# Masked attention block on one core: inverse roots placed apart from their scalings, Q or K ahead of three output projections, V finished in slot 4, and a quarter of the square moves made by ScalarE

## Chip, core and metric

The kernel runs on one core of a Trainium2 chip. The metric is device microseconds of one execution. The engines are named as in the profile: PE (TensorE), PEld (its weight loads), DVE (VectorE), ACT (ScalarE), POOL (GpSimd), SP (SyncE, which issues all DMAs here).

## The reference, cut to what matters

```python
# x: (8, 1024, 384) f32, adj: (8, 1024, 1024) bool, 6 heads of 64
q = heads(x @ Wq + bq); k = heads(x @ Wk + bk); v = heads(x @ Wv + bv)
scores = einsum('bhqd,bhkd->bhqk', q, k) / sqrt(64)
probs = softmax(scores + where(adj, 0.0, -9e15), axis=-1)
ctx = einsum('bhqk,bhkd->bhqd', probs, v)          # merged to (8, 1024, 384)
out = layernorm(x + ctx @ Wf + bf)                  # over the last axis, no affine
```

## The kernel before

Products of full precision are made as three products of a high and a low part in F32R (`three_products`). Each batch (1024 tokens) is cut into 24 slots. A slot `s` makes the scores of one block of 128 queries against all 1024 keys for one pair of heads. Two slots (an even and the following odd one) make a group: 256 queries, one pair of heads; a batch has 12 groups, and three groups (the three pairs of heads) make one row block of 256 tokens.

In a slot PE writes the scores of two heads to `score_ps` (`scores`). DVE adds the mask and finds the row minimum (`mask_scores`, two instructions, one for each head; the text calls the first of them the slot's mask), ACT takes the exponential in place in `prob` (`exponential`), and DVE transposes each 32x32 block in place (`turn_squares`). For the product with V the whole matrix has to be transposed, so after the group's odd slot the 4x4 squares of 32 partitions by 1024 elements are moved from `prob` to `prob_t`, from partitions 32a to partitions 32c (`move_square`, 16 DMAs for a group; `move` issues them in two halves). Each adds 16 to the semaphore `landed[group % 2]`; at 256 the group is complete. Both buffers are double: group g uses half g % 2. So the mask of the next slot that writes that half, slot 2g+4, waits for `landed`, and so does `mix(g)`.

`mix(g)` (32 products on PE into `context_ps`, which line 514 of the profile shows) stands in slot 2g+4, except that group 0 comes in slot 5. Before it stands job `i`: PE spreads the inverted row sums over a PSUM bank (line 436) and ACT copies them to `context`, ahead of the slot's exponentials (`evicted_early`). After the mix DVE multiplies (`divide`), ACT rounds to the high part (`context_high`, line 612), POOL forms the low part (`context_low`, line 805); the output projection `p` of a tile needs these.

What PE does in each slot beside the scores is written out by hand in the table `STEADY`: `("kind", number, piece, ahead)`, with kinds `q`, `k`, `v` (projections), `x` (transposes of the next batch's x), `i`, `m` (mix) and `p` (output projection). `ahead` 1 is work for the next batch, a negative number belongs to the batch before. Jobs take three PSUM banks in turn (`bank_free`). ACT evicts the jobs in the same order behind the exponentials: for `q`, `k` and `x` a high part and a copy `raw` (two halves in turn), from which POOL forms the low part (`low_part`). All engines run the same table in order, each waiting on semaphores. Other tables say in which slot SP loads and stores (`STORES`, `RES_LOADS`, `X_LOADS`), where POOL adds the bias to the residual rows (`RESIDUALS`), and where POOL normalises (`NORMALISE`): there `normalise` makes 12 small steps for the inverse root and then `scale_rows` two instructions of 128x384, at the end of POOL's work of the slot.

Of the kernel before, what the change touches and what calls it, by code (L numbers as in the profile page):

```python
# [11 lines left out]
ACT = mybir.ActivationFunctionType  # L12
# [8 lines left out]
ROOT_OPS = 4 * NEWTON_STEPS  # L21
# [41 lines left out]

STORES = {1: -2, 9: -1, 13: 0, 19: 1}
RES_LOADS = {2: 0, 10: 1, 14: 2, 20: 3}
X_LOADS = {4: (0, 0), 6: (0, 1), 11: (1, 0), 12: (1, 1)}
RESIDUALS = {6: 0, 13: 1, 17: 2, 23: 3}
NORMALISE = {0: -2, 8: -1, 12: 0, 18: 1}

# [25 lines left out]
def slots_of(mode):  # L95
    return range(SLOTS + 2 if mode == "last" else SLOTS)


def evicted_early(mode, s):

    jobs = [w for w in slot_work(mode, s) if w[0] != "m"]
    return jobs[:1] if jobs and (jobs[0][0] == "i" or s == 5) else []


def contexts_split(mode, s):

    groups = [w[1] for w in slot_work(mode, s) if w[0] == "m" and SPLIT_LATER.get(s) != w[1]]
    return [SPLIT_LATER[s - 1]] + groups if s - 1 in SPLIT_LATER else groups


# [6 lines left out]
def graph_attention(nc, x, adj, wq, bq, wk, bk, wv, bv, wf, bf, out):  # L117
# [15 lines left out]
    with ExitStack() as ctx:  # L133
# [181 lines left out]
        def _(sp):  # L315
# [26 lines left out]
            def move(b, group, part):  # L342
                if part == 0:
                    sp.wait_ge(squared, at(b, UNITS, 4 * group + 4))
                    sp.wait_ge(mixed, at(b, GROUPS, group + 1))
                for a in (2 * part, 2 * part + 1):
                    for c in range(4):
                        move_square(sp, group, a, c)

# [207 lines left out]
        def _(act):  # L557
# [42 lines left out]
            def exponential(b, t):  # L600
# [6 lines left out]
                                     accum_out=row_sum[:, s // 2 % 2, col:col + 1]).then_inc(exp_done, 1)  # L607

            def context_high(b, group):
                act.wait_ge(context_done, at(b, GROUPS, group + 3))  # L610
                act.wait_ge(projected, at(b, TT, 2 * ((group - 4) // 3) + 6))
                nc.scalar.activation(context_hi[:, group % 4, :], context[:], ACT.Copy).then_inc(context_hi_done, 1)  # L612

            def body(b):
                for s in slots_of(b.mode):
                    early = evicted_early(b.mode, s)
                    for job in early:
                        evict(b, job)
                    if s < SLOTS:
                        exponential(b, 2 * s)  # L620
                        exponential(b, 2 * s + 1)
                    if s - 1 in SPLIT_LATER:
                        context_high(b, SPLIT_LATER[s - 1])
                    for job in slot_work(b.mode, s):
                        if job[0] not in "pm" and job not in early:
                            evict(b, job)
                    for group in contexts_split(b.mode, s):
                        if s - 1 not in SPLIT_LATER:
                            context_high(b, group)
# [17 lines left out]
        def _(dve):  # L647
# [71 lines left out]
            def body(b):  # L719
                for s in slots_of(b.mode):  # L720
# [11 lines left out]
                    for job in work:  # L732
                        if job[0] == "p":
                            add_residual(b, job)
                            moments(b, job[1])

            weights = 0
# [27 lines left out]
        def _(pool):  # L765
# [41 lines left out]

            def normalise(b, group):
                pool.wait_ge(guess_done, at(b, 4, group + 1))
# [9 lines left out]
                for _ in range(NEWTON_STEPS):  # L819
# [3 lines left out]
                    result(nc.gpsimd.tensor_tensor(guess, guess, newton[:], ALU.mult))  # L823
                scale_rows(nc.gpsimd, group)

            def body(b):
                for s in slots_of(b.mode):
                    work = slot_work(b.mode, s)
                    for job in work:
# [9 lines left out]
                    for group in contexts_split(b.mode, s):  # L839
                        context_low(b, group)  # L840
                    if s in RESIDUALS:
                        residual(b, RESIDUALS[s])
                    if s in NORMALISE and (NORMALISE[s] >= 0 or b.mode != "first"):
                        normalise(b, NORMALISE[s])
                    if s == SLOTS:
                        normalise(b, 2)
                    if s == SLOTS + 1:
                        normalise(b, 3)

# [35 lines left out]
```

## Time and profile before

| what | value |
|---|---|
| median of 3 runs | 1355.2 us (1343.33 to 1359.98) |
| profiled execution | 1353.83 us, its span 1352.0 us |
| PE busy | 1196.9 us, 89% |
| DVE busy | 1057.4 us, 78% |
| ACT busy | 736.7 us, 54% |
| POOL busy | 654.4 us, 48% |
| DMA queue of SP | 111488 packets, 250.13 MB, 76.7% of 16 engines |

The busy times are sums over the whole span. The first of the eight batches is filled while the weights are prepared, and the last has no next batch to work for; the six between repeat the same pattern, so one of them (a stretch of 162.9 us) stands for all. The span and the execution's time differ by 1.83 us.

### The profile page before, as it was taken

How to read it: one execution, taken by the hardware profiler on the slowest of the kernel's cores; microseconds unless marked ns; L12 is line 12 of the kernel's file. 1: busy time of each engine (PE TensorE's matmuls, PEld its weight loads, DVE VectorE, ACT ScalarE, POOL GpSimd, SP SyncE). 2: the span in 40 equal slices, each digit the busy share in tenths (PEclk: the TensorE clock that was granted, in tenths of full speed). 3: DMA queues.
4: the chain of work that ended last, by engine and by line, in shares of the span. 5: the costliest groups of instructions: out<-in, count | busy, mean ns of one | idle time of the engine just before them, and what ended most of it. 6: DMA issues, size and time to landing. Idle time of an engine off the chain costs nothing.

```text
span 1352.0 us, 23753 instructions
## 1 busy us (share of the span) xinstructions
PE 1196.9 (89%) x8406; PEld 889.4 (66%) x8406; DVE 1057.4 (78%) x1617; ACT 736.7 (54%) x1404; POOL 654.4 (48%) x958
## 2 busy tenths in 40 slices
PE   7998899888998889888899898998899888998873
PEld 5765677656776667666677666766577666776542
DVE  5788777887778877788777888688877887779881
ACT  5655555555555656466455555555655555554540
POOL 1235562545625555375544664445643555624534
PEclk9999999998999999999898998999999999999987
DMA  4688867788678877788787887789867897678873
GB/s 154 161 190 213 189 159 191 190 221 192 153 190 199 223 181 177 184 207 201 170 199 173 212 191 183 177 188 224 193 152 190 199 228 185 162 170 196 204 185 86
DMA packets 111607, 251.66 MB, mean 186 GB/s; under 512 B 27904, under 2 KB 62336, under 8 KB 111488
## 3 DMA queue, kind: packets, MB, share of 16 engines
q1 hardware_dynamic: 111488, 250.13, 76.7%
q8 instruction: 67, 1.10, 0.4%
q14 instruction: 52, 0.43, 0.1%
HBM read 36.11 MB, written 12.58 MB: 36 GB/s over the span
## 4 chain that ended last, share of the span: by engine, by line
PE 51%; DVE 16%; SPq 11%; ACT 7%; POOL 7%; issue 5%; DMA 3%; POOLq 0%; ACTq 0%; DVEq 0%
PE context_ps L514 14%; PE score_ps L499 12%; SPq L306 10%; PE job_ps L405 8%; DVE prob L682 7%; PE job_ps L406 7%; PE job_ps L407 7%; ACT prob L605 5%; DVE prob L675 5%; DMA prob_t<-prob 2%; PE job_ps L436 2%; POOL res L300 2%; POOL context_lo L805 1%; POOL xt_lo L789 1%; DVE stats L706 1%
## 5 line engine op out<-in xcount | busy, mean ns | idle before, releaser
L675 DVE CUSTOM_DVE_ANT_0 prob<-score_ps,mask 128x1024 f32<-128x1024 f32 x384 | 454.5, 1220 | 169.0 <-PE score_ps L499 141.8
L605 ACT ACTIVATE prob<-prob,row_min 128x1024 f32<-128x1024 f32 x384 | 440.5, 1149 | 210.2 <-DVE row_min L675 210.1
L682 DVE STREAM_TRANSPOSE prob<-prob 128x1024 f32<-128x1024 f32 x384 | 458.5, 1232 | 75.9 <-ACT prob L605 75.9
L514 PE MATMUL context_ps<-prob_t,v_all 128*64 128x256 f32 x3072 | 356.5, 385 | 43.5 <-DMA prob_t<-prob 38.1
L514 PEld LDWEIGHTS context_ps<-prob_t,v_all 128*64 128x64 f32 x3072 | 232.7, 139 | 153.2 <-issue 60.1
L499 PE MATMUL score_ps<-k_hi,q_hi 64*128 64x512 f32 x768 | 141.6, 446 | 16.2 <-DVE row_min L675 16.2
L805 POOL TENSOR_TENSOR context_lo<-context,context_hi 128x256 fp32r<-128x256 f32 x96 | 70.6, 735 | 171.6 <-ACT context_hi L612 171.6
L771 POOL TENSOR_SCALAR mask<-adj_in 128x1024 f32<-128x1024 uint8 x64 | 67.0, 1046 | 170.8 <-DVE row_min L675 157.7
L793 POOL TENSOR_TENSOR q_lo<-raw,q_hi 128x256 fp32r<-128x256 f32 x95 | 69.3, 734 | 164.0 <-ACT raw L597 162.3
L405 PE MATMUL job_ps<-xt_hi,weight_hi 128*128 128x256 f32 (+1 forms) x423 | 143.3, 339 | 0.0
L406 PE MATMUL job_ps<-xt_lo,weight_hi 128*128 128x256 f32 (+1 forms) x423 | 138.4, 327 | 0.0
L407 PE MATMUL job_ps<-xt_hi,weight_lo 128*128 128x256 f32 (+1 forms) x423 | 138.1, 326 | 0.0
L405 PE MATMUL job_ps<-weight_hi,context_hi 128*128 128x384 f32 x192 | 77.1, 402 | 64.0 <-POOL context_lo L805 64.0
L499 PE MATMUL score_ps<-k_lo,q_hi 64*128 64x512 f32 x768 | 121.0, 392 | 0.0
L499 PE MATMUL score_ps<-k_hi,q_lo 64*128 64x512 f32 x768 | 120.5, 390 | 0.0
L612 ACT ACTIVATE context_hi<-context 128x256 fp32r<-128x256 f32 x96 | 40.1, 417 | 126.6 <-DVE context L692 126.6
L793 POOL TENSOR_TENSOR k_lo<-raw,k_hi 128x512 fp32r<-128x512 f32 x46 | 58.3, 1282 | 102.7 <-ACT raw L597 102.7
L300 POOL TENSOR_SCALAR res<-res,mean_var,inv_dev 128x384 f32<-128x384 f32 x64 | 105.0, 1647 | 3.5
L597 ACT ACTIVATE raw<-job_ps,bias_qk 128x256 f32<-128x256 f32 (+1 forms) x141 | 75.9, 538 | 56.2 <-POOL q_lo L793 32.6
L799 POOL TENSOR_TENSOR diag<-ident,inv_sum 128x512 f32<-128x512 f32 x96 | 100.0, 1042 | 10.5 <-DVE inv_sum L687 7.4
L499 PEld LDWEIGHTS score_ps<-k_hi,q_hi 64*128 64x128 f32 x768 | 57.7, 186 | 69.6 <-issue 36.4
L405 PEld LDWEIGHTS job_ps<-xt_hi,weight_hi 128*128 128x128 f32 x423 | 82.9, 196 | 21.3 <-issue 14.2
(72 smaller groups left out, 1700.9 us busy)
## 6 DMA issues: line engine op xcount, KB each, us to landing
prob_t<-prob SPq DMA_DIRECT2D x1536, 128.0 KB, 2.4
res<-in_x_dram SPq DMA_DIRECT2D x32, 384.0 KB, 3.9
out_dram<-res SPq DMA_DIRECT2D x32, 384.0 KB, 2.9
x_in<-in_x_dram SPq DMA_DIRECT2D x30, 384.0 KB, 3.8
adj_in<-in_adj_dram SPq DMA_DIRECT2D x31, 256.0 KB, 3.1
res<-in_x_dram SPq DMA_DIRECT2D x1, 768.0 KB, 6.7
prob_t<-in_L_gnn_Wk_dram SPq DMA_DIRECT2D x1, 576.0 KB, 4.0
prob_t<-in_L_gnn_Wq_dram SPq DMA_DIRECT2D x1, 576.0 KB, 8.1
```

The source lines that it names most:

```text
L300: engine.tensor_scalar(res[:, n, :], res[:, n, :], mean_var[:, group % 2, tile, 0:1], inv_dev[:, group % 2, tile:tile + 1], ALU.subtract, ...
L306: queue.dma_start(prob_t[32 * c:32 * c + 32, group % 2, a].rearrange("p q h n -> p (q h n)"), prob[32 * a:32 * a + 32, group % 2, c].rearr ...
L405: pe.matmul(dst, left_hi, right_hi, start=(t == 0), stop=False)
L406: pe.matmul(dst, left_hi, right_lo, start=False, stop=False)
L407: last = pe.matmul(dst, left_lo, right_hi, start=False, stop=(t == FT - 1))
L499: last[head] = pe.matmul(score_ps[:, head, keys], q_part[rows, pair, q], k_part[rows, pair, keys], start=(n == 0), stop=(n == 2))
L514: last = pe.matmul(context_ps[64 * head:64 * head + 64, 0:GQ], v_all[:, kt, col:col + HS], keys, start=(kt == 0), stop=(kt == TT - 1))
L605: nc.scalar.activation(probabilities(t), probabilities(t), ACT.Exp, scale=-1.0, bias=row_min[:, ring:ring + 1], accum_out=row_sum[:, s // ...
L675: nc.vector.tensor_tensor_reduce(probabilities(t), in_quarters(score_ps[:, head, :]), in_quarters(mask[:, s % 2, :]), 1.0, HUGE, ALU.add, ...
L682: nc.vector.transpose(probabilities(t), probabilities(t)).then_inc(squared, 1)
L793: nc.gpsimd.tensor_tensor(lo, copy[:, 0:width], hi, ALU.subtract).then_inc(lo_done, 1)
L799: nc.gpsimd.tensor_tensor(diag[:], ident[:].unsqueeze(1).to_broadcast([P, 4, P]), inv_sum[:, group % 2, :].unsqueeze(2).to_broadcast([P, 4 ...
```

## The change

The tables and six places in the code change.

- A square with a = c stays on its partitions. SP no longer issues these four of a group's 16 moves; ACT copies them (`keep_square`, 32 partitions by 1024 elements, `prob` to `prob_t`), two in slot 2g+2 and two in slot 2g+3, behind the evictions and ahead of `context_high`. Each adds 16 to `landed`, so the mask of slot 2g+4 and `mix(g)` now wait for ACT too.
- `normalise` is divided: `find_root` stands at the head of POOL's slot (`ROOTS`), `scale_rows` at its end (`SCALINGS`); group 1 is scaled in slot 19 instead of 18. Its store and the next load move two slots on (21 and 22), and the residual rows of group 3 are prepared in slot 2 of the next batch instead of slot 23.
- In slots 9 and 15 the `q` stands ahead of the `p`, in slot 21 the `k`.
- The eight V projections stand 2, 3, 3 in slots 2 to 4 (before 1, 3, 3, 1 in slots 2 to 5), and `i` of group 0 moves from slot 4 to slot 5.
- At the very end DVE, not POOL, scales the last two tiles.

The diff, cut to its core:

```diff
-    2: [("i", -1, 0, 0), ("m", -1, 0, 0), ("v", 0, 0, 0)],
-    3: [("v", 1, 0, 0), ("v", 2, 0, 0), ("v", 3, 0, 0)],
-    4: [("i", 0, 0, 0), ("v", 4, 0, 0), ("v", 5, 0, 0), ("v", 6, 0, 0)],
-    5: [("v", 7, 0, 0), ("m", 0, 0, 0)],
+    2: [("i", -1, 0, 0), ("m", -1, 0, 0), ("v", 0, 0, 0), ("v", 1, 0, 0)],
+    3: [("v", 2, 0, 0), ("v", 3, 0, 0), ("v", 4, 0, 0)],
+    4: [("v", 5, 0, 0), ("v", 6, 0, 0), ("v", 7, 0, 0)],
+    5: [("i", 0, 0, 0), ("m", 0, 0, 0)],
...
-    21: [("p", 4, 0, 0), ("k", 1, 0, 1)],
+    21: [("k", 1, 0, 1), ("p", 4, 0, 0)],
...
-STORES = {1: -2, 9: -1, 13: 0, 19: 1}
-RES_LOADS = {2: 0, 10: 1, 14: 2, 20: 3}
+STORES = {1: -2, 9: -1, 13: 0, 21: 1}
+RES_LOADS = {2: 0, 10: 1, 14: 2, 22: 3}
...
-RESIDUALS = {6: 0, 13: 1, 17: 2, 23: 3}
-NORMALISE = {0: -2, 8: -1, 12: 0, 18: 1}
+RESIDUALS = {2: -1, 6: 0, 13: 1, 17: 2}
+ROOTS = {0: -2, 8: -1, 12: 0, 18: 1, 24: 2}
+SCALINGS = {0: -2, 8: -1, 12: 0, 19: 1, 24: 2}
...
+def own_squares(s):
+
+    if s >= SLOTS:
+        return range(4) if s == SLOTS else ()
+    return (2 * (s % 2), 2 * (s % 2) + 1)
...
                 for a in (2 * part, 2 * part + 1):
                     for c in range(4):
-                        move_square(sp, group, a, c)
+                        if c != a:
+                            move_square(sp, group, a, c)
...
+            def keep_square(b, group, a):
+                act.wait_ge(squared, at(b, UNITS, 4 * group + 4))
+                act.wait_ge(mixed, at(b, GROUPS, group + 1))
+                own = slice(32 * a, 32 * a + 32)
+                nc.scalar.activation(prob_t[own, group % 2, a].rearrange("p q h n -> p (q h n)"),
+                                     prob[own, group % 2, a].rearrange("p q h n -> p (q h n)"),
+                                     ACT.Copy).then_inc(landed[group % 2], 16)
...
                     for job in slot_work(b.mode, s):
                         if job[0] not in "pm" and job not in early:
                             evict(b, job)
+                    if s >= 2 or b.mode != "first":
+                        for a in own_squares(s):
+                            keep_square(b, s // 2 - 1, a)
...
+                    if s == SLOTS + 1:
+                        dve.wait_ge(root_ops, at(b, 4 * ROOT_OPS, 4 * ROOT_OPS))
+                        scale_rows(nc.vector, 3)
...
+                    if s in ROOTS and (ROOTS[s] >= 0 or b.mode != "first"):
+                        find_root(b, ROOTS[s])
...
-                    if s in NORMALISE and (NORMALISE[s] >= 0 or b.mode != "first"):
-                        normalise(b, NORMALISE[s])
+                    if s in SCALINGS and (SCALINGS[s] >= 0 or b.mode != "first"):
+                        scale_rows(nc.gpsimd, SCALINGS[s])
```

ACT in slots 15 and 16 of a middle batch, before (`prob` are the exponentials, `context<-job_ps` the eviction of `i`):

```order
L605 ACTIVATE prob,row_sum<-prob,row_min 128x4x256 [waits masked] x2
L590 ACTIVATE q_hi<-job_ps,bias_qk 128x256 [waits job_done]
L597 ACTIVATE raw<-job_ps,bias_qk 128x256 [waits lo_done]
L580 ACTIVATE context<-job_ps 128x256 [waits context_lo_done,job_done]
L605 ACTIVATE prob,row_sum<-prob,row_min 128x4x256 [waits masked] x2
L612 ACTIVATE context_hi<-context 128x256 [waits projected,context_done]
```

The same place of the changed kernel:

```order
L614 ACTIVATE prob,row_sum<-prob,row_min 128x4x256 [waits masked] x2
L599 ACTIVATE q_hi<-job_ps,bias_qk 128x256 [waits job_done]
L606 ACTIVATE raw<-job_ps,bias_qk 128x256 [waits lo_done]
L622 ACTIVATE prob_t<-prob 32x1024 [waits mixed,squared] x2
L589 ACTIVATE context<-job_ps 128x256 [waits context_lo_done,job_done]
L614 ACTIVATE prob,row_sum<-prob,row_min 128x4x256 [waits masked] x2
L622 ACTIVATE prob_t<-prob 32x1024 [waits mixed,squared] x2
L629 ACTIVATE context_hi<-context 128x256 [waits projected,context_done]
```

Two copies stand between the evictions of slot 15 and the eviction of slot 16's `i`, and two more ahead of `context_high`.

POOL in slots 18 to 20 of a middle batch, before, from the low parts of slot 18's two `x` on (of the twelve steps of the root the first and the last stand here):

```order
L789 TENSOR_TENSOR xt_lo<-raw,xt_hi 128x2x8x32 x2
L799 TENSOR_TENSOR diag<-ident,inv_sum 128x512
L805 TENSOR_TENSOR context_lo<-context,context_hi 128x256
L820 TENSOR_TENSOR newton<-inv_dev 128x2
...
L823 TENSOR_TENSOR inv_dev<-inv_dev,newton 128x2
L300 TENSOR_SCALAR res<-res,mean_var,inv_dev 128x384 x2
L793 TENSOR_TENSOR q_lo<-raw,q_hi 128x256
L793 TENSOR_TENSOR k_lo<-raw,k_hi 128x512 x2
L799 TENSOR_TENSOR diag<-ident,inv_sum 128x512
```

And of the changed kernel:

```order
L843 TENSOR_TENSOR newton<-inv_dev 128x2
...
L846 TENSOR_TENSOR inv_dev<-inv_dev,newton 128x2
L812 TENSOR_TENSOR xt_lo<-raw,xt_hi 128x2x8x32 x2
L822 TENSOR_TENSOR diag<-ident,inv_sum 128x512
L828 TENSOR_TENSOR context_lo<-context,context_hi 128x256
L816 TENSOR_TENSOR q_lo<-raw,q_hi 128x256
L816 TENSOR_TENSOR k_lo<-raw,k_hi 128x512 x2
L308 TENSOR_SCALAR res<-res,mean_var,inv_dev 128x384 x2
L822 TENSOR_TENSOR diag<-ident,inv_sum 128x512
```

The root has gone ahead of the low parts of `x`, and the scaling behind the low parts of slot 19's `q` and `k`.

## Rows read from the trace of the kernel before

**Rows 1.** The page: busy time of PE, and the chain that ended last by engine

```profile
PE 1196.9 (89%) x8406; PEld 889.4 (66%) x8406; DVE 1057.4 (78%) x1617; ACT 736.7 (54%) x1404; POOL 654.4 (48%) x958
PE 51%; DVE 16%; SPq 11%; ACT 7%; POOL 7%; issue 5%; DMA 3%; POOLq 0%; ACTq 0%; DVEq 0%
```

**Rows 2.** Busy time by stretch (engines in order), then granted clock, DMA share, GB/s

```profile
535.90:698.80 162.90, 147.21 (x1053) 109.22 (x1052) 130.56 (x202) 91.93 (x176) 83.07 (x120) 0.98 0.79 191
652.50:658.70 6.20, 6.20 (x20) 5.30 (x20) 4.52 (x8) 2.17 (x4) 0.00 (x0) 0.59 0.63 174
```

**Rows 3.** Who waited for whom: us in total, times, longest

```profile
PE context_ps L514 <- DMA prob_t<-prob: 38.1, 20, 9.0
```

**Rows 4.** PE by time, slots 14, 21, 22: start, us, instructions [idle before <-releaser]

```profile
604.73 3.67 PE L514 MATMUL context_ps<-prob_t,v_all 128*64 128x256 f32 x32 [2.82 <-DMA prob_t<-prob]
...
652.50 0.66 PE L405 MATMUL job_ps<-weight_hi,context_hi 128*128 128x384 f32 x1 [4.24 <-POOL context_lo L805]
...
658.65 0.73 PE L499 MATMUL score_ps<-k_hi,q_hi 64*128 64x512 f32 x4
```

**Rows 5.** SP's queue by time, first half of the squares after slot 11

```profile
590.12 5.88 SPq L306 DMA_DIRECT2D prob_t<-prob  x8
```

**Rows 6.** DVE by time: the masks of slots 13, 14 and 15

```profile
597.25 1.21 DVE L675 CUSTOM_DVE_ANT_0 prob<-score_ps,mask 128x1024 f32<-128x1024 f32 x1
...
604.73 1.23 DVE L675 CUSTOM_DVE_ANT_0 prob<-score_ps,mask 128x1024 f32<-128x1024 f32 x1 [2.50 <-DMA prob_t<-prob]
...
610.04 1.23 DVE L675 CUSTOM_DVE_ANT_0 prob<-score_ps,mask 128x1024 f32<-128x1024 f32 x1
```

**Rows 7.** ACT by time: evictions in slots 13, 18, 19 and 1

```profile
600.80 0.46 ACT L590 ACTIVATE q_hi<-job_ps,bias_qk 128x256 fp32r<-128x256 f32 x1
...
601.51 0.47 ACT L590 ACTIVATE q_hi<-job_ps,bias_qk 128x256 fp32r<-128x256 f32 x1
...
633.60 0.58 ACT L586 ACTIVATE xt_hi<-job_ps 128x512 fp32r<-128x512 f32 x1
...
634.55 0.60 ACT L586 ACTIVATE xt_hi<-job_ps 128x512 fp32r<-128x512 f32 x1
...
646.29 0.69 ACT L597 ACTIVATE raw<-job_ps,bias_qk 128x512 f32<-128x512 f32 x1 [4.54 <-POOL q_lo L793]
...
682.95 0.67 ACT L590 ACTIVATE k_hi<-job_ps,bias_qk 128x512 fp32r<-128x512 f32 x1
...
684.09 0.69 ACT L590 ACTIVATE k_hi<-job_ps,bias_qk 128x512 fp32r<-128x512 f32 x1
```

**Rows 8.** POOL by time, the scaling in slot 18

```profile
642.28 3.28 POOL L300 TENSOR_SCALAR res<-res,mean_var,inv_dev 128x384 f32<-128x384 f32 x2
```

**Rows 9.** ACT's groups by shape: busy us, mean ns | idle before, releaser

```profile
L605 ACT ACTIVATE prob<-prob,row_min 128x1024 f32<-128x1024 f32 x384 | 440.5, 1149 | 210.2 <-DVE row_min L675 210.1
...
L612 ACT ACTIVATE context_hi<-context 128x256 fp32r<-128x256 f32 x96 | 40.1, 417 | 126.6 <-DVE context L692 126.6
...
L634 ACT ACTIVATE weight_hi<-prob_t 128x1152 fp32r<-128x1152 f32 x4 | 4.6, 1158 | 2.8 <-DMA prob_t<-in_L_gnn_Wk_dram 2.8
```

**Rows 10.** ACT by time at the start: a copy of 1152 elements, its successor

```profile
16.29 1.15 ACT L634 ACTIVATE weight_hi<-prob_t 128x1152 fp32r<-128x1152 f32 x1
17.34 0.68 ACT L568 ACTIVATE k_hi<-score_ps,bias_qk 128x512 fp32r<-128x512 f32 x1
```

**Rows 11.** PE by time: V projections of slot 3, then slot 4's scores

```profile
693.82 0.45 PE L405 MATMUL job_ps<-weight_hi,xt_hi 128*128 128x384 f32 x1
...
698.74 0.73 PE L499 MATMUL score_ps<-k_hi,q_hi 64*128 64x512 f32 x4
```

**Rows 12.** DVE by time, last batch: the masks of slots 9 and 23

```profile
1224.83 1.21 DVE L675 CUSTOM_DVE_ANT_0 prob<-score_ps,mask 128x1024 f32<-128x1024 f32 x1
...
1313.12 1.22 DVE L675 CUSTOM_DVE_ANT_0 prob<-score_ps,mask 128x1024 f32<-128x1024 f32 x1 [1.16 <-PE score_ps L499]
```

**Rows 13.** PE by time, the last mix

```profile
1330.06 5.30 PE L514 MATMUL context_ps<-prob_t,v_all 128*64 128x256 f32 x32 [8.96 <-DMA prob_t<-prob]
```

More of the change, by code:

```diff
@@ L101, in evicted_early @@
     jobs = [w for w in slot_work(mode, s) if w[0] != "m"]
-    return jobs[:1] if jobs and (jobs[0][0] == "i" or s == 5) else []
+    return jobs[:1] if jobs and jobs[0][0] == "i" else []
 def contexts_split(mode, s):
@@ L806, in context_low, with find_root @@
                                         ALU.subtract).then_inc(context_lo_done, 1)
-            def normalise(b, group):
+            def find_root(b, group):
                 pool.wait_ge(guess_done, at(b, 4, group + 1))
@@ L823, in normalise @@
                     result(nc.gpsimd.tensor_tensor(guess, guess, newton[:], ALU.mult))
-                scale_rows(nc.gpsimd, group)
             def body(b):
                 for s in slots_of(b.mode):
+                    if s == SLOTS:
+                        residual(b, 3)
+                    if s in ROOTS and (ROOTS[s] >= 0 or b.mode != "first"):
+                        find_root(b, ROOTS[s])
                     work = slot_work(b.mode, s)
@@ L840, in body @@
                         context_low(b, group)
-                    if s in RESIDUALS:
+                    if s in RESIDUALS and (RESIDUALS[s] >= 0 or b.mode != "first"):
                         residual(b, RESIDUALS[s])
-                    if s in NORMALISE and (NORMALISE[s] >= 0 or b.mode != "first"):
-                        normalise(b, NORMALISE[s])
-                    if s == SLOTS:
-                        normalise(b, 2)
+                    if s in SCALINGS and (SCALINGS[s] >= 0 or b.mode != "first"):
+                        scale_rows(nc.gpsimd, SCALINGS[s])
                     if s == SLOTS + 1:
-                        normalise(b, 3)
+                        find_root(b, 3)
             nc.gpsimd.memset(ident[:], 0.0).then_inc(ident_clear, 1)
```

4 rows, old and new, of the table STEADY are left out of this document.

## The prediction

> **What bounds the kernel now.** I read the page's busy times first, then one steady batch, then who stops PE in it. PE is busy 89% of the span, and the chain that ended last is half PE and half a walk over DVE, SP's queue, ACT and POOL [rows 1]: PE sets the pace, and what can be won is its idle time. A middle batch takes 162.9 us with 147.2 of PE work and 91.9 of ACT work [rows 2], so at most 15.7 us a batch, 9.6%, can go.
>
> PE by time shows where it stands. In slot 14 the mix waits 2.82 us for moved squares [rows 4], and the mask of that slot waits 2.50 for the same [rows 6]; all such waits of the mix sum to 38.1 us [rows 3]. SP explains it: the first eight squares after slot 11 take 5.88 us [rows 5], 0.73 each, so 16 take 11.8 us, and that is nearly the whole time that two slots last. In slot 21 the projection waits 4.24 us, and then the granted clock is 0.59, the lower of the two levels (1.2 GHz), for most of 6.2 us [rows 2, 4]. Its cause lies two slots back: POOL scales rows for 3.28 us [rows 8] ahead of the low parts of slot 19, ACT's copy `raw` waits 4.54 us for them until 646.29 [rows 7], and the exponentials of slot 20 stand behind that copy.
>
> **The squares.** SP issues 12 instead of 16, so the last one goes 2.9 us earlier (4 x 0.73). Counted from the end of the odd slot's transposes, 12 issues and one load make 9.5 us, plus landing; the mask that needs them comes some 13 us later, so the DMA waits go. Their place can be taken by ACT's copies. No row shows a copy of 1024 elements from SBUF to SBUF. A copy of 1152 takes 1.158 us and one of 256 takes 0.417 [rows 9], which gives 1.05 on the line between them; the next instruction starts 0.10 before the end (16.29 + 1.15 against 17.34, [rows 10]). So a copy occupies ACT 0.95 us and a pair has landed 2.0 us after its start. The bounds: 0.85, if only the slope of these two rows counts, and 1.15, the exponential on as many elements [rows 9]. I take 0.95, since the rows on both sides of it are the same operation. 48 copies add 46 us to ACT's 91.9 in a batch: still below 162.9, but the place in ACT's order decides, not the sum.
>
> **ACT's new chain.** Call K the time when the copies of an odd slot end. The mask of the next even slot and its mix start just after K (+0.1), as both need all 16 squares. From that mask to the mask of the following odd slot it is 5.31 us (604.73 to 610.04, a case where mask and mix also start together, [rows 6]), from an odd slot's mask until ACT is through with both exponentials 3.55 us (597.25 to 600.80, [rows 6, 7]). Then come the slot's evictions, e, and 2.0 us of copies. So K to K takes 10.95 + e. The evictions cost 0.7 us for a `q`, 0.95 for an `x`, 1.15 for a `k` (601.51 - 600.80, 634.55 - 633.60, 684.09 - 682.95, [rows 7]). Pair by pair, named by its odd slot:
>
> slot 9 (q, x): 12.6, and 0.6 since the moments of two tiles hold DVE in slot 7: 13.2. Slot 11 (q, x): 12.6, and 0.3 since ACT, after slot 10's `x` and copies, comes late to the exponentials: 12.9. Slot 13 (q, q): 12.4. Slot 15 (q): 11.7. Slot 17 (q, x): 12.6. Slot 19 (q, k, k): 13.95, and 1.2 since two `x` and two copies of slot 18 run into slot 19: 15.15. Slot 21 (k): 12.1. Slot 23 (k, q): 12.8, and 0.35 for a `q` that PE makes last: 13.15. Slot 1 (k, k, q): 13.95, 1.1 for slot 0's `q` behind the mix, and 0.85 for a `raw` that waits for POOL's scaling: 15.9. Slots 3 and 5 follow PE: after the mix two V's, then three, then three, at 1.64 each (4.92 for the three of slot 3 until slot 4's scores start, [rows 11]), and K comes 16.0 and 11.6 later. Slot 7: 13.8, since its `q` stands behind two projections. The sum is 160.5 us against 162.9: **2.4 us a batch**.
>
> So the larger part of the gain is given back. In slot 14 the mix would start at 604.95, by this chain, where it now starts at 604.73: ACT's copies take the very place of the squares that SP brought late. After slot 13's exponentials end, two `q` (1.4) and two copies (2.0) stand in front of it. The waits of the mix for copies come to 2.5 us in slots 14 and 20 and 2.4 in slot 2, and about 1 in slots 8, 10, 12, 16, 22 and 0.
>
> **Root, scaling and order.** The root of group 1 runs at the head of slot 18, while PE mixes; the scaling follows the low parts of slot 19, and the next that POOL owes (diagonal and low part of the context in slot 20) is due some 3 us after it ends. So this costs nothing, and the 4.54 us at ACT and the 4.24 us at PE go, with the 2.5 us that the lower clock adds in slot 21 (0.41 of 6.2 us). The scores of slot 22, which start at 658.65 [rows 4], would start 5.2 us earlier; the K's of slots 23 to 3 eat most of that. In slots 9, 15 and 21 the `q` or `k` fills a wait for `context_lo`; this is in the sum, as PE then waits for K instead. If the scaling were late, slot 20's `context_low` would be, and the cost returns up to 3.28 us a batch. The residual of group 3, store 1 and its load move into stretches where POOL and SP have nothing due; they count as nothing, and if SP were held by the wait for store 1, six squares of slot 21 would be late by that wait. The V's order alone costs nothing: it is the same PE work.
>
> **Ends.** From slot 7 of the first batch to slot 7 of the last there are seven periods: 7 x 2.4 = 17. In the last batch without work ahead the masks of slots 9 to 23 lie 88.3 us apart [rows 12]; with e = 0.7 or nothing the chain gives 11.7 a pair, 12.2 where DVE's moments of two tiles count, 82.7 in all: 5.6 us. At the very end the last mix, at the lower clock, waits 8.96 us for squares [rows 13]; four issues less (4 x 0.73) bring it 2.9 us forward. The last two scalings go from POOL, 3.28 us as in [rows 8], to DVE, whose nearest row, the mask, takes 1.2 us for 1024 elements [rows 6], so about 0.45 for 384, 0.9 for two: 2.4 less. The sum: 17 + 5.6 + 2.9 + 2.4 = 27.9. From the span of 1352.0 that leaves 1324.1, with the 1.83 around it 1326. The profiled execution, 1353.83, lies 1.4 below the median of the three, 1355.2; this is noise, and I forecast **1326 us**, 2.1% below either.
>
> **The rivals.** *The clock falls at the new waits: slower.* After the wait of 2.82 us in slot 14 the 32 products took 3.67 us [rows 4], after the one of 8.96 they took 5.30 [rows 13], and after 4.24 the clock was at its lower level [rows 2]. My waits of 2.4 to 2.5 us lie just below the first of these. If three mixes a batch run at the lower level, each costs 1.6 us more, and the next K as much: 3 x 8 x 1.6 = 38, 1364 us, slower than before. It decides from the point where PE, having waited, is granted 1.2 GHz. The Trainium skill, in "TensorE: Matmul & The Clock Gate", part 1 (The HAM clock gate), says that "the default state is throttled, and activity releases the throttle"; by that rule more scattered waiting speaks against this change, and the trace agrees for slot 21 and not for slot 14. Chance 0.13.
>
> *The copies cost what an exponential does*, 1.15: each 0.1 us on a copy is 0.2 us in each pair but the two that follow PE, 2 us a batch and 17 in the run, so +34: 1360, no difference that can be told. For it speaks that the shape uses 32 partitions, which no row shows; against it both copy rows. Chance 0.10. At 0.85 the same gives 1309; chance 0.15.
>
> *POOL's root at the head of the slot waits for the moments* (`guess_done`), with the low parts, diagonal and context behind it. If this reaches PE by 2 us in slots 18 and 0, 8 x 4 = 32 come back: 1358. Against it: POOL works 83.1 us of 162.9 in a batch [rows 2]. Chance 0.12.
>
> *SP alone was the brake and ACT's copies are hidden.* Then only the small waits for sums and projections remain, about 4.5 us beside 147.2: 11 us a batch, 77 in seven, with the ends 1266. Against it stands ACT's strict order, exponentials and evictions ahead of the copies. Chance 0.05.
>
> **How the numbers follow.** The forecast has 0.45. The range 1303 to 1355 takes in both bounds of the copy as far as 0.82 and 1.12 us and part of POOL's case, and leaves out the clock and the 1266. A measurement of this kernel tells about 2% from no change, here 1328 on one side and 1382 on the other. Faster by over 2%: half of the forecast's 0.45, all of the cheap copies and of the last rival, and a little of the rest: 0.47. Slower by over 2% needs the clock and a dear copy together: 0.06. Within 2%: 0.47.
>
> **What would show it.** In the profile after, rows of ACT's copy at 1.05 us, 384 of them; the wait of the mix in slots 14, 20 and 2 put down to ACT, not DMA; no wait of 4 us for `context_lo` in slot 21 and no stretch at 0.59 behind it; a period of 160.5 us. The prediction is wrong if the period stays at 163 or above (then look at the clock behind the mixes), or if it falls to 155 (then mask and mix don't wait for the copies, and the chain from K to K is shorter than I have it).

## The result, and the profile after

The changed kernel takes **1387.1 us** (median of 4 runs, 1385.7 to 1389.6); the kernel before, run beside it, 1350.6 (1343.3 to 1360.0). The ratio is 1.027, 95% interval 1.019 to 1.034: slower, though not surely by as much as 2%, where 1326 us and a range up to 1355 were forecast.

The page after, for [rows 1]: busy time, the chain that ended last, and the group of the copies.

```profile
PE 1212.7 (88%) x8406; PEld 902.1 (65%) x8406; DVE 1061.2 (77%) x1619; ACT 1128.4 (81%) x1788; POOL 652.3 (47%) x956
...
ACT 36%; PE 32%; DVE 11%; issue 10%; POOL 8%; DMA 1%; SPq 1%; ACTq 0%; DVEq 0%; POOLq 0%
...
L622 ACT ACTIVATE prob_t<-prob 32x1024 f32<-32x1024 f32 x384 | 404.0, 1052 | 7.2
```

SP's queue has all but left the chain (11% before, 1% now) and ACT has gone from 7% to 36%. A copy lasts 1.052 us, as read off the line between two other shapes.

Who waited for whom after, for [rows 3]: us in total, times, longest.

```profile
DVE prob L695 <- ACT prob_t L622: 138.8, 75, 4.6
PE context_ps L523 <- ACT prob_t L622: 124.2, 87, 3.7
DVE prob L702 <- ACT prob L614: 54.4, 192, 1.7
PE job_ps L414 <- POOL context_lo L828: 11.4, 12, 1.9
...
PE context_ps L523 <- DMA prob_t<-prob: 1.6, 1, 1.6
```

The mix waited 38.1 us for moved squares before; it waits 1.6 now, and 124.2 for ACT's copies. The wait of the projections for `context_lo` has shrunk to 11.4; before it was

```profile
PE job_ps L405 <- POOL context_lo L805: 64.0, 25, 4.6
```

Slots 17 to 21 of a middle batch, then the whole batch from slot 2's mix to the next, for [rows 2] (same columns):

```profile
641.00:675.00 34.00, 30.22 (x211) 22.27 (x207) 26.80 (x41) 30.82 (x50) 22.16 (x31) 1.00 0.54 126
541.39:708.89 167.50, 149.24 (x1050) 111.49 (x1051) 130.86 (x201) 140.77 (x225) 83.20 (x121) 0.98 0.61 148
```

The batch takes 167.5 us, not 160.5; others take up to 170.8. The stretch in which slot 21 held the lower clock runs at 1.00 here, so that step of the change works.

PE by time after, for [rows 4]: the mixes of slots 2, 14, 16, 18 and 20 of that batch, and of the next slot 14.

```profile
541.39 5.36 PE L523 MATMUL context_ps<-prob_t,v_all 128*64 128x256 f32 x32 [2.20 <-ACT prob_t L622]
...
624.63 5.07 PE L523 MATMUL context_ps<-prob_t,v_all 128*64 128x256 f32 x32 [2.73 <-ACT prob_t L622]
637.99 3.67 PE L523 MATMUL context_ps<-prob_t,v_all 128*64 128x256 f32 x32 [1.67 <-ACT prob_t L622]
650.94 3.67 PE L523 MATMUL context_ps<-prob_t,v_all 128*64 128x256 f32 x32 [0.48 <-ACT prob_t L622]
666.55 3.67 PE L523 MATMUL context_ps<-prob_t,v_all 128*64 128x256 f32 x32 [2.65 <-ACT prob_t L622]
...
792.16 6.62 PE L523 MATMUL context_ps<-prob_t,v_all 128*64 128x256 f32 x32 [2.73 <-ACT prob_t L622]
```

The waits stand where the prediction put them, nearly at its lengths (2.20 in slot 2, 2.73 and 2.65 in slots 14 and 20). But the same 32 products take 3.67 us after one such wait and 5.0 to 6.6 after another. Over the whole run 19 of the 96 mixes lie at the lower clock, 4 before. Two of these four are from slot 14 of the kernel before, in other batches than the one of [rows 4]:

```profile
932.73 5.36 PE L514 MATMUL context_ps<-prob_t,v_all 128*64 128x256 f32 x32 [2.90 <-DMA prob_t<-prob]
...
1094.47 5.33 PE L514 MATMUL context_ps<-prob_t,v_all 128*64 128x256 f32 x32 [1.90 <-DMA prob_t<-prob]
```

ACT by time after, for [rows 7]: from slot 12's copies to slot 14's `i`.

```profile
615.47 2.12 ACT L622 ACTIVATE prob_t<-prob 32x1024 f32<-32x1024 f32 x2
617.62 0.42 ACT L629 ACTIVATE context_hi<-context 128x256 fp32r<-128x256 f32 x1
...
621.85 0.48 ACT L606 ACTIVATE raw<-job_ps,bias_qk 128x256 f32<-128x256 f32 x1
622.36 2.13 ACT L622 ACTIVATE prob_t<-prob 32x1024 f32<-32x1024 f32 x2
624.51 0.38 ACT L589 ACTIVATE context<-job_ps 128x256 f32<-128x256 f32 x1
```

DVE by time, for [rows 6]: the masks of slots 13 to 15.

```profile
617.23 1.23 DVE L695 CUSTOM_DVE_ANT_0 prob<-score_ps,mask 128x1024 f32<-128x1024 f32 x1
...
624.63 1.23 DVE L695 CUSTOM_DVE_ANT_0 prob<-score_ps,mask 128x1024 f32<-128x1024 f32 x1 [2.41 <-ACT prob_t L622]
...
631.32 1.23 DVE L695 CUSTOM_DVE_ANT_0 prob<-score_ps,mask 128x1024 f32<-128x1024 f32 x1 [1.16 <-PE score_ps L508]
```

Two copies and their neighbours follow one another without overlap: the pair starts 0.03 after `raw` ends, lasts 2.13 instead of 2.0, and the next starts 0.02 after it. Mask and mix of slot 14 start together, 0.14 after the copies end.

### The profile page after: what moved, and what is told of

Its sections match the earlier page's. It is cut to its first block, busy times and chain, and to the rows that moved or that the text cites. A ratio compares the mean times of both kernels' runs of the same rounds, so it can differ in the third digit from the quotient of the medians.

```text
span 1385.8 us, 24152 instructions
## 1 busy us (share of the span) xinstructions
PE 1212.7 (88%) x8406; PEld 902.1 (65%) x8406; DVE 1061.2 (77%) x1619; ACT 1128.4 (81%) x1788; POOL 652.3 (47%) x956
## 4 chain that ended last, share of the span: by engine, by line
ACT 36%; PE 32%; DVE 11%; issue 10%; POOL 8%; DMA 1%; SPq 1%; ACTq 0%; DVEq 0%; POOLq 0%
PE context_ps L523 17%; ACT prob_t L622 17%; ACT prob L614 10%; PE score_ps L508 6%; DVE prob L695 5%; DVE prob L702 4%; PE job_ps L414 3%; ACT raw L606 3%; POOL res L308 3%; PE job_ps L416 3%; PE job_ps L415 3%; POOL context_lo L828 2%; ACT q_hi L599 1%; ACT xt_hi L595 1%; ACT raw L604 1%
## 5 line engine op out<-in xcount | busy, mean ns | idle before, releaser
L702 DVE STREAM_TRANSPOSE prob<-prob 128x1024 f32<-128x1024 f32 x384 | 458.3, 1232 | 54.4 <-ACT prob L614 54.4
L523 PE MATMUL context_ps<-prob_t,v_all 128*64 128x256 f32 x3072 | 389.6, 410 | 125.8 <-ACT prob_t L622 124.2
L523 PEld LDWEIGHTS context_ps<-prob_t,v_all 128*64 128x64 f32 x3072 | 269.4, 148 | 242.0 <-issue 169.9
L622 ACT ACTIVATE prob_t<-prob 32x1024 f32<-32x1024 f32 x384 | 404.0, 1052 | 7.2
L415 PE MATMUL job_ps<-xt_lo,weight_hi 128*128 128x256 f32 (+1 forms) x423 | 135.5, 320 | 0.0
L308 POOL TENSOR_SCALAR res<-res,mean_var,inv_dev 128x384 f32<-128x384 f32 x62 | 101.8, 1649 | 0.0
L414 PEld LDWEIGHTS job_ps<-xt_hi,weight_hi 128*128 128x128 f32 x423 | 79.4, 188 | 29.1 <-issue 22.4
L416 PEld LDWEIGHTS job_ps<-xt_hi,weight_lo 128*128 128x128 f32 x423 | 79.6, 188 | 6.6
L508 PEld LDWEIGHTS score_ps<-k_hi,q_lo 64*128 64x128 f32 x768 | 72.8, 185 | 16.5
```

The source lines that it names most:

```text
L308: engine.tensor_scalar(res[:, n, :], res[:, n, :], mean_var[:, group % 2, tile, 0:1], inv_dev[:, group % 2, tile:tile + 1], ALU.subtract, ...
L414: pe.matmul(dst, left_hi, right_hi, start=(t == 0), stop=False)
L415: pe.matmul(dst, left_hi, right_lo, start=False, stop=False)
L416: last = pe.matmul(dst, left_lo, right_hi, start=False, stop=(t == FT - 1))
L508: last[head] = pe.matmul(score_ps[:, head, keys], q_part[rows, pair, q], k_part[rows, pair, keys], start=(n == 0), stop=(n == 2))
L523: last = pe.matmul(context_ps[64 * head:64 * head + 64, 0:GQ], v_all[:, kt, col:col + HS], keys, start=(kt == 0), stop=(kt == TT - 1))
```

## The experiments

Ratios are to the kernel before, timed beside each (1346.9 to 1350.6 us), with their 95% intervals.

**1. The change without its copies.** SP moves all 16 squares.

```diff
-                        if c != a:
-                            move_square(sp, group, a, c)
+                        move_square(sp, group, a, c)
...
-                        for a in own_squares(s):
-                            keep_square(b, s // 2 - 1, a)
```

> The changed kernel with all 16 squares of a group on SP again and no copies on ACT; tables, roots and scalings stay as changed. Theory (the loss comes from ACT's copies standing ahead of the mask and the mix; the rest of the change helps): the waits of the mix for ACT vanish, slot 21's wait of 4.2 us stays away, the batch takes 158 to 161 us, 1325 to 1340 us in all, faster than before. Rival (the new order of jobs and POOL's roots at the head of slots cost the time): 1375 us or more.

Measured: 1301.1 us, 0.966 (0.963 to 0.968), below the 1325 to 1340 expected. So roots, order and V's gain 47 us, and the copies as placed cost 86. The mix waits 46.2 us in all for SP's squares:

```profile
PE context_ps L522 <- DMA prob_t<-prob: 46.2, 27, 5.2
```

**2. The copies alone**, in the kernel before (`own_squares`, `keep_square` and `if c != a` added).

```diff
+                        if c != a:
+                            move_square(sp, group, a, c)
...
+                        for a in own_squares(s):
+                            keep_square(b, s // 2 - 1, a)
```

> The kernel before with the copies on ACT alone; tables, normalisation and order as before. Theory: the same chain through ACT, and in addition the wait behind POOL's scaling in slots 19 to 21: slower than the changed kernel, 1390 to 1420 us. Rival (the order costs the time): about as before, 1340 to 1360 us.

Measured: 1482.1 us, 1.100 (1.097 to 1.103); mean granted clock 0.945. The copies cost 134 us in the old order, far more than expected: the new one takes up a part of their price.

**3. Only the first copy of a group waits** for `squared` and `mixed`, so those of an odd slot carry no wait, to see whether the waits keep a copy from overlapping.

```diff
-                act.wait_ge(squared, at(b, UNITS, 4 * group + 4))
-                act.wait_ge(mixed, at(b, GROUPS, group + 1))
+                if a == 0:
+                    act.wait_ge(squared, at(b, UNITS, 4 * group + 4))
+                    act.wait_ge(mixed, at(b, GROUPS, group + 1))
```

> The changed kernel, but of a group's four copies only the first carries the two waits (the others follow it on the same engine, so they need none). Theory (a copy with two waits of its own does not overlap with the instruction before it, which makes a pair 2.13 us after a gap where I had reckoned 2.0): a pair of copies in an odd slot takes 1.95 to 2.0 us, K to K 0.2 to 0.3 us less, 2.4 to 3.6 us a batch, 1355 to 1368 us. Rival (the copies take 1.05 us each whatever they wait for): within 0.5% of the changed kernel, 1380 to 1390 us.

Measured: 1384.7 us, 1.028 (1.023 to 1.033), a pair still 2.13. The waits are not what keeps copies apart.

**4. PE kept busy ahead of the late mixes.** In slots 2, 14 and 20 PE makes 16 products more, into columns of `context_ps` that nobody reads; PE would have waited there.

```diff
+FILLED = (-1, 5, 8)
+FILLS = 16
...
+                if group in FILLED:
+                    for n in range(FILLS):
+                        pe.matmul(context_ps[:, GQ:2 * GQ], weight_hi[:, 0, 0, 0:P], weight_hi[:, 0, 1, 0:GQ],
+                                  start=True, stop=True)
```

> The changed kernel with 16 products more (128x256, into the unused half of the context bank) ahead of the mix in slots 2, 14 and 20, where PE waits 2.2 to 2.7 us for ACT. Theory (the lower clock behind these waits costs 1.7 us in slot 2 and up to 2.9 in slots 14 and 20): the mix there takes 3.7 us in every batch, 3.5 to 4 us less a batch, 1355 to 1362 us. Rival (ACT's chain sets the pace whatever the mix takes): within 0.5% of 1387 us.

Measured: 1359.0 us, 1.008 (1.005 to 1.011), mean clock 0.990 against 0.968. With more work, the kernel is 28 us faster than the changed one (25 by the ratios): this is what the lower clock behind these three waits cost. PE by time, slot 12's mix (which has no filler), the filler and slot 14's mix, and that mix a batch later:

```profile
600.71 5.36 PE L531 MATMUL context_ps<-prob_t,v_all 128*64 128x256 f32 x32 [1.51 <-ACT prob_t L630]
...
612.31 2.17 PE L521 MATMUL context_ps<-weight_hi 128*128 128x256 f32 x16
615.02 3.67 PE L531 MATMUL context_ps<-prob_t,v_all 128*64 128x256 f32 x32 [0.54 <-ACT prob_t L630]
...
779.27 3.67 PE L531 MATMUL context_ps<-prob_t,v_all 128*64 128x256 f32 x32 [0.55 <-ACT prob_t L630]
```

The period here is 164.25 us (165.9 where slot 12's mix runs at the lower clock), and 4 of 96 mixes are left at it. The copies' pace has not changed: the chain without the clock still is 3.7 us a batch above 160.5.

**5. In the odd slot the copies go ahead of the evictions**, straight behind the exponentials (with the waits on a group's first copy alone, as in 3).

```diff
+                    keeps = own_squares(s) if s >= 2 or b.mode != "first" else ()
+                    if s % 2 == 1:
+                        for a in keeps:
+                            keep_square(b, s // 2 - 1, a)
...
+                    if s % 2 == 0:
+                        for a in keeps:
```

> The changed kernel, but in odd slots ACT makes the two copies straight after the exponentials, ahead of the evictions (and only the first copy of a group waits). Theory (the time lies in the chain from mask over exponentials, evictions and copies to the next mask and mix): the evictions drop out of that chain, 0.7 to 3 us in nine of twelve pairs; the waits of the mix for ACT fall below 1 us and the lower clock behind them goes; a batch takes 156 to 161 us, 1310 to 1345 us in all. Rival (ACT's added load of 46 us a batch costs the time wherever it stands): 1370 us or more.

Measured: 1305.7 us, 0.969 (0.967 to 0.971), 81 below the changed kernel and just below the range expected; clock 0.991, period 157.5 to 158.3. Some 28 of the 81 are the clock of experiment 4, the rest a shorter chain. Of 124.2 us that the mix waited for copies 18.0 are left:

```profile
PE context_ps L523 <- ACT prob_t L623: 18.0, 13, 3.7
DVE prob L700 <- ACT prob_t L623: 9.9, 10, 1.3
```

Nothing was removed: the evictions, e in the prediction's chain, need only come out from between the exponentials and the copies.

**6. The copies add 1 to a semaphore of their own**, instead of 16 to `landed`, to see whether the increment keeps copies apart.

```diff
-                                     ACT.Copy).then_inc(landed[group % 2], 16)
+                                     ACT.Copy).then_inc(kept[group % 2], 1)
```

> The changed kernel, but a copy adds 1 to a semaphore of its own, not 16 to the one of the DMAs; mask and mix wait for both. Theory (the increment by 16 keeps a copy from overlapping with its neighbours, which makes K to K 0.3 us longer than reckoned): a pair of copies takes 2.0 us and starts before the instruction ahead of it ends, 1355 to 1370 us. Rival (something else about the copy, such as its 32 partitions, keeps it apart): a pair stays at 2.13 us, 1378 to 1392 us.

Measured: 1386.2 us, 1.028 (1.025 to 1.032), a pair 2.12 to 2.13. The increment is not the cause either.

**7. Only the two copies of the even slot**; SP moves the other 14.

```diff
-    return (2 * (s % 2), 2 * (s % 2) + 1)
+    return (0, 1) if s % 2 == 0 else ()
...
-                        if c != a:
+                        if c != a or a >= 2:
```

> The changed kernel with two copies of a group only, those of the even slot; the squares of the odd slot's copies go by SP, which issues 14 of 16. Theory (copies in even slots lie in time in which ACT waits for the product anyway, those in odd slots stand ahead of mask and mix): no wait of the mix for ACT is left, the waits for DMA are shorter than with 16 squares, 1283 to 1300 us, as fast as 16 by SP (1301) or faster. Rival (each copy costs its share of the 86 us between 1387 and 1301): about 1344 us.

Measured: **1266.1 us**, 0.941 (0.938 to 0.944), below both kernels and below the 1283 to 1300 expected. The two copies are hidden and relieve SP; the mix waits 24.2 us for squares against 46.2 in experiment 1, and for ACT not at all. ACT by time in an even slot:

```profile
612.00 2.13 ACT L622 ACTIVATE prob_t<-prob 32x1024 f32<-32x1024 f32 x2
614.15 0.42 ACT L629 ACTIVATE context_hi<-context 128x256 fp32r<-128x256 f32 x1
615.32 1.15 ACT L614 ACTIVATE prob<-prob,row_min 128x1024 f32<-128x1024 f32 x1 [0.76 <-DVE row_min L695]
```

Behind copies and high part ACT still waits 0.76 for the next minimum: there was a hole, time in which ACT would have waited anyway.

**8. Roots, scalings and stores alone**, with the old order of PE's jobs and SP moving all squares.

```diff
-NORMALISE = {0: -2, 8: -1, 12: 0, 18: 1}
+ROOTS = {0: -2, 8: -1, 12: 0, 18: 1, 24: 2}
+SCALINGS = {0: -2, 8: -1, 12: 0, 19: 1, 24: 2}
...
```

> The kernel before with roots and scalings apart (with their store, load and residual, and DVE's last scaling), 16 squares by SP, the order of the jobs as before. Theory (the wait in slot 21 with the lower clock behind it is most of what the tables win): slot 21's wait goes, 4 to 5 us a batch, 1310 to 1322 us. Rival (Q and K ahead of projections and the V's win most of it): 1330 to 1350 us.

Measured: 1311.8 us, 0.975 (0.972 to 0.978): some 35 of experiment 1's gain is here, the order of jobs, V's among them, makes the other 12. From the mix of slot 20 to that of slot 22 it is now 12.2 us in each middle batch, where it was 16.9 to 18.1.

**9. What keeps copies apart: the partitions.** Twelve ACT copies more at the very end, with both buffers dead: three of 128 partitions; two on 0 to 63, one on 64 to 127; two on 0 to 31, then 32 to 63, 64 to 95, 96 to 127; last 64 to 127. The kernel took 1389.0 us in its one run; only the distances between the starts count here.

```diff
+            probe(slice(0, 128), 0, 0)
+            probe(slice(0, 128), 0, 1)
...
+            probe(slice(64, 128), 0, 3)
+            probe(slice(0, 32), 1, 2)
+            probe(slice(0, 32), 1, 3)
+            probe(slice(32, 64), 1, 2)
...
```

> The changed kernel with twelve more ACT copies of 1024 elements at its very end, when both buffers are dead: three of 128 partitions, three of 64, then five of 32 (two on the same partitions, three on changing ones) and one of 64. Only the distances between starts count. If narrow copies don't run into their successors, the three of 128 start 1.06 us apart, as the exponentials do, and those of 32 start 1.07 to 1.09 apart with 1.05 each; the 64's then tell whether any narrowing does it. If copying from SBUF to SBUF is what prevents it, those of 128 are as far apart as their duration too. If it is the change of partitions, only the last three of 32 are.

ACT by time there, from the second on (start, us):

```profile
1373.21 1.04 ACT L666 ACTIVATE prob_t<-prob 128x1024 f32<-128x1024 f32 x1
1374.16 1.04 ACT L666 ACTIVATE prob_t<-prob 128x1024 f32<-128x1024 f32 x1
1375.11 1.04 ACT L666 ACTIVATE prob_t<-prob 64x1024 f32<-64x1024 f32 x1
1376.05 1.04 ACT L666 ACTIVATE prob_t<-prob 64x1024 f32<-64x1024 f32 x1
1377.11 1.05 ACT L666 ACTIVATE prob_t<-prob 64x1024 f32<-64x1024 f32 x1
1378.17 1.06 ACT L666 ACTIVATE prob_t<-prob 32x1024 f32<-32x1024 f32 x1
1379.14 1.04 ACT L666 ACTIVATE prob_t<-prob 32x1024 f32<-32x1024 f32 x1
1380.19 1.05 ACT L666 ACTIVATE prob_t<-prob 32x1024 f32<-32x1024 f32 x1
1381.25 1.05 ACT L666 ACTIVATE prob_t<-prob 32x1024 f32<-32x1024 f32 x1
1382.32 1.05 ACT L666 ACTIVATE prob_t<-prob 32x1024 f32<-32x1024 f32 x1
1383.38 1.05 ACT L666 ACTIVATE prob_t<-prob 64x1024 f32<-64x1024 f32 x1
```

A copy that begins on the same partition as the one ahead starts 0.94 to 0.97 after it (1374.16, 1375.11, 1376.05, 1379.14); one that begins on another starts 1.05 to 1.07 after it (1377.11, 1378.17, 1380.19, 1381.25, 1382.32, 1383.38). The width doesn't decide it: two of 32 partitions overlap as those of 128 do. In an odd slot `keep_square` begins at partition 64 and then at 96, behind and ahead of instructions that begin at 0, and so loses this 0.1 three times.

**10. All four copies in the even slot.**

```diff
-    return (2 * (s % 2), 2 * (s % 2) + 1)
+    return range(4) if s % 2 == 0 else ()
```

> The changed kernel with all four copies of a group in the even slot, none in the odd one. If the place decides (a copy costs only where it stands between an odd slot's exponentials and the next mask), four copies take 4.25 us behind slot 14's exponentials, where ACT idles 1.83 before the next ones after two of them: the odd exponentials come some 0.3 to 0.5 us late in a slot without evictions and 1 to 2 in one with an eviction, so 1270 to 1300 us, below the 1305.65 with the odd slot's copies put first. If the number of copies decides, wherever they stand, it is 1305 or above.

Measured: 1416.7 us, 1.050 (1.044 to 1.055); clock 0.946. The expectation from the place fell: that only the odd slot costs is wrong. The other, 1305 or above, gave no reason for 111 us more than that. No mix waits for ACT, but the odd slot's exponentials come late, and DVE's transposes wait for them 218.4 us (54.4 in the changed kernel):

```profile
637.98 4.28 ACT L622 ACTIVATE prob_t<-prob 32x1024 f32<-32x1024 f32 x4
642.28 0.42 ACT L629 ACTIVATE context_hi<-context 128x256 fp32r<-128x256 f32 x1
642.61 1.13 ACT L614 ACTIVATE prob<-prob,row_min 128x1024 f32<-128x1024 f32 x1
```

The exponential follows with no wait for its minimum: the hole is overfull. The projection waits 78.3 us for `context_lo` as well (20.7 in experiment 7), more than PE waits for anything else here: the high part stands behind all four copies. Experiment 11 was to tell the two apart.

**11 and 12. `context_high` ahead of the copies**, with four in the even slot (11) and with two (12).

```diff
+                    for group in contexts_split(b.mode, s):
+                        if s - 1 not in SPLIT_LATER:
+                            context_high(b, group)
                     if s >= 2 or b.mode != "first":
                         for a in own_squares(s):
                             keep_square(b, s // 2 - 1, a)
-                    for group in contexts_split(b.mode, s):
-                        if s - 1 not in SPLIT_LATER:
-                            context_high(b, group)
```

> All four copies in the even slot, with context_high ahead of them. If the late high part is what makes that kernel slow (the projection waits up to 4.3 us for context_lo, 78 us in all), most of this comes back: 1340 to 1375 us, and the wait for context_lo falls below 25 us. If the lateness of the odd slot's exponentials behind four copies is (DVE's transposes wait 1.9 us for them in every odd slot), it stays at 1400 or above, since a high part that itself waits for the mix puts the copies later still.

> Two copies in the even slot alone, with context_high ahead of them. If two copies there are hidden, as their run at 1266.14 suggests, the order of the two changes little: 1255 to 1280 us. If they hold back the low part and the projection there too, it falls below 1250; if the wait for the mix ahead of the copies makes the next exponentials late, it rises above 1285.

Measured: 11, 1494.3 us, 1.108 (1.105 to 1.112); the wait for `context_lo` falls to 23.8 us, but the transposes wait 317.7 for exponentials. 12, 1318.9 us, 0.977 (0.974 to 0.981), 53 above experiment 7. ACT by time in 12:

```profile
635.77 0.42 ACT L629 ACTIVATE context_hi<-context 128x256 fp32r<-128x256 f32 x1 [1.62 <-DVE context L712]
636.10 2.13 ACT L622 ACTIVATE prob_t<-prob 32x1024 f32<-32x1024 f32 x2
638.25 1.15 ACT L614 ACTIVATE prob<-prob,row_min 128x1024 f32<-128x1024 f32 x1
```

ACT's wait for the product of mix and division, in experiments 1, 7 and 12:

```profile
ACT context_hi L628 <- DVE context L708: 122.1, 67, 9.4
...
ACT context_hi L629 <- DVE context L712: 27.0, 11, 8.5
...
ACT context_hi L629 <- DVE context L712: 120.1, 77, 9.8
```

So the hole is ACT's wait for mix and product of the even slot. Two copies ahead of `context_high` fill it; behind it they delay the exponentials. What made experiment 10 slow is not settled: experiment 11 mends the late high parts and by the same move puts the copies, and so the exponentials, later still. It shows that the kernel is no faster with the high parts in time, not what share the exponentials had in 10.

## Why the prediction was wrong

**Right: roots, SP and where the waits would stand.** The wait of 4.24 us and the 0.59 behind it are gone; slot 22 gains some 5.4 us a batch in experiment 8, 5.2 reckoned. The DMA waits went, ACT took their place, and the waits in slots 14, 20 and 2 have the lengths that the chain gave. The projections' wait for `context_lo` fell from 64.0 to 11.4 us, so the rival of POOL's root fell.

**Wrong: "My waits of 2.4 to 2.5 us lie just below the first of these."** From one wait of 2.82 us in slot 14 that kept the clock I inferred that shorter ones would, and gave the falling clock 0.13. The same slot two and three batches later shows mixes of 5.36 and 5.33 after 2.90 and 1.90; I had read one batch of eight. In its first seven batches the kernel before has such a wait in slot 14 each time, of 1.7 to 3.0 us, and two of the seven mixes behind them run at the lower clock. In the changed kernel a 2.20 cost the clock and a 2.65 did not, so the length of the wait just ahead doesn't sort the cases. The 19 mixes at the lower level take 36.9 us more than 19 of 3.67, the 4 of experiment 4 6.4 more: 30 us apart, and experiment 4 measured 28. The rival's size, 38, came near, though by errors that partly cancel (24 mixes at 1.6 us reckoned, 19 at 1.9 measured); its chance was wrong. The period of 163 or above that was to show the forecast wrong came.

**Off in size: "a copy occupies ACT 0.95 us and a pair has landed 2.0 us after its start."** The duration was right, the overlap of 0.10 was taken from a row where both instructions span all partitions [rows 10]. The copies of an odd slot, which end K, begin on other partitions than their neighbours, and experiment 9 shows that such copies don't overlap. It makes 1.06 a copy: a pair takes 2.13 and starts 0.13 later, 0.26 a pair. Twelve pairs give 3.1 of the 3.7 us by which the undisturbed batch of experiment 4, 164.25, exceeds 160.5. The prediction charged a dearer copy to ten pairs only, as slots 3 and 5 follow PE; from mask to mask in that batch these two are 0.25 and 0.29 us longer as well. The others are 0.2 to 0.7 longer than listed, but for slot 9's, which is 0.4 shorter. The bounds, 0.82 to 1.12, held the copy's 1.06.

**The account.** 1387.1 less 1326 is 61, and it all lies in the seven periods. From the mask of slot 7 in the first batch to the one in the last it is 1139.1 us in the kernel before, so 1122 by the forecast of 17 less; it is 1183.2 after and 1154.2 in experiment 4. So 29 are the clock that experiment 4 gives back, 26 the chain's pace, seven times 3.7, and 5 the three mixes that still run at the lower clock there (5.36 instead of 3.67). At the ends errors cancel: the masks of slots 9 to 23 of the last batch take 85.8 us, not 82.7, but what follows the last mix is 4.0 shorter than before, not 2.4, and the first batch reaches slot 7 1.1 earlier. The case "the clock and a dear copy together", which had 0.06, is nearest to what came, with a copy at 1.06, about halfway from 0.95 to the 1.15 of that case.

**What the forecast had no view of.** It took the change as one and found the gain given back. In truth its parts pull apart: 47 us gained without the copies (experiment 1), 86 lost by them. Their price is one of place and number: 81 of it comes back by order alone (experiment 5), and two copies in ACT's hole bring 35 us more than none (experiment 7). That run ends at the 1266 of the last rival by coincidence, with two copies, not four: four were not hidden in any place that was tried.

## What to carry to other kernels

Work given to an engine that runs in strict order costs by what stands behind it and by what it stands behind: look for a place where that engine waits anyway, measure how long it waits, and put no more there than fits; here 2.1 us fitted and 4.3 did not. Where a step rests on "the clock stays up after such a wait", read that place in every batch, not in one. A change of several parts may hold a gain and a loss that are both larger than its sum, so price each part against the others left out.

## What was not expected of the hardware

ACT's instructions overlap by about 0.10 us if they begin on the same partition (starts 0.94 to 0.97 apart at 1.04 to 1.06 each; experiment 9, copies of 32, 64 and 128 partitions), and not at all if that partition changes (1.05 to 1.07 apart, copies of 32 and 64). The Trainium skill, "ScalarE: Activation LUTs", section "What ACT_TABLE_LOAD costs", says beside its figures for a tile of 128 partitions that ACTIVATEs one behind the other overlap by some 93 ns. The measurement agrees for the first case; in the second, which that section doesn't treat, there is no overlap.

The granted clock after a wait could not be told from that wait alone: 3.67 us for 32 products after 2.65, 5.36 after 2.20, 5.36 after 1.51 in experiment 4. What else decides it stays open. Sixteen products of 2.17 us put into the wait kept the mixes behind it at the higher of the two levels.
